# Flamingo block, two gated layers: first Toeplitz tiles read from the taps, a third buffer for turned x, weight signs spread out and moved, down products of the last stage one tile later

## The reference

```
x = x + tanh(g_xattn[0]) * conv_attention(ctx, ctx, layernorm(x))
x = x + tanh(g_ffn[0])   * ffn_A(layernorm(x))    # hidden 1408
x = x + tanh(g_xattn[1]) * attention(layernorm(x), ctx, mask)
x = x + tanh(g_ffn[1])   * ffn_B(layernorm(x))    # hidden 2048
```

## Time and profile before

| | |
|---|---|
| three runs | 777.58, 780.79, 781.33 us, median 780.79 |
| the profiled execution | 780.78 us, span 779.0 us, granted clock 0.976 of 2.4 GHz |
| TensorE | 709.3 us busy, 91% of the span |
| VectorE | 619.5 us, 80% |
| ScalarE | 373.4 us, 48% |
| GpSimd | 245.3 us, 31% |
| chain that ended last | TensorE 58%, VectorE 26%, issue 5%, ScalarE 4%, DMA 4% |

### The profile page before, as it was taken

How to read it: one execution, slowest core, us unless ns; L and a number is a source line. 1 busy time by engine, 2 the same in 40 slices (tenths; PEclk the granted TensorE clock), 3 DMA queues, 4 the chain that set the end, 5 groups by cost and what they waited for, 6 DMA issues and landing times.

```text
span 779.0 us, 9462 instructions
## 1 busy us (share of the span) xinstructions
PE 709.3 (91%) x3160; PEld 391.5 (50%) x3160; DVE 619.5 (80%) x1216; ACT 373.4 (48%) x541; POOL 245.3 (31%) x299
## 2 busy tenths in 40 slices
PE   3999999987989999977988989999999999999975
PEld 2767767765634444445654434444444444444431
DVE  1888988787989999754877698888888888888860
ACT  3154865354167778744764153334444444444430
POOL 5477687786545444232421001000000000000000
PEclk9999999999999999998999999999999999999996
DMA  7473273131049999979521034544443444333323
GB/s 258 143 269 123 61 268 117 70 93 35 7 121 220 227 204 150 218 203 318 178 82 28 1 68 81 82 82 81 82 77 73 81 82 69 74 74 65 68 60 81
DMA packets 140080, 90.97 MB, mean 117 GB/s; under 512 B 118848, under 2 KB 118848, under 8 KB 140032
## 3 DMA queue, kind: packets, MB, share of 16 engines
q1 hardware_dynamic: 138320, 86.01, 46.2%
q0 software_dynamic: 1280, 4.20, 1.8%
q10 hardware_dynamic: 432, 0.17, 0.2%
HBM read 53.04 MB, written 8.47 MB: 79 GB/s over the span
## 4 chain that ended last, share of the span: by engine, by line
PE 58%; DVE 26%; issue 5%; ACT 4%; DMA 4%; POOL 2%; SPq 1%; ACTq 0%; POOLq 0%; DVEq 0%
PE psum L732 27%; PE psum L749 14%; PE psum L614 10%; DVE phase_space L1020 3%; PE psum L693 3%; DVE phase_space L1068 3%; DVE phase_space L1029 2%; DVE a_scalars L1074 2%; DVE psum L1022 2%; DVE ln_bn L273 2%; PE psum L715 2%; DMA phase_space<-in_L_weights 2%; DVE a_scalars L1050 1%; DMA phase_space<-phase_space 1%; DVE phase_space L1035 1%
## 5 line engine op out<-in xcount | busy, mean ns | idle before, releaser
L732 PE MATMUL psum<-phase_space 128*128 128x512 f16 x1024 | 224.1, 379 | 2.8 <-DVE phase_space L1167 2.8
L614 PE MATMUL psum<-phase_space 128*128 128x288 f32 x640 | 168.7, 417 | 15.3 <-ACT phase_space L812 15.3
L732 PEld LDWEIGHTS psum<-phase_space 128*128 128x128 f16 x1024 | 100.1, 98 | 124.6 <-DVE phase_space L1167 3.8
L614 PEld LDWEIGHTS psum<-phase_space 128*128 128x128 f32 x640 | 121.1, 195 | 52.0 <-ACT phase_space L812 21.7
L749 PE MATMUL psum<-phase_space 128*128 128x512 f16 x512 | 116.0, 386 | 9.4 <-DMA phase_space<-phase_space 9.4
L589 POOL DMA_DIRECT2D out<-x_sb x16 | 9.5, 593 | 334.7 <-DVE x_sb L1200 334.7
L749 PEld LDWEIGHTS psum<-phase_space 128*128 128x128 f16 x512 | 50.7, 99 | 72.2 <-issue 13.7
L659 PE MATMUL psum<-phase_space 128*128 128x512 bf16 (+1 forms) x384 | 81.0, 366 | 5.4 <-DVE phase_space L1068 4.4
L982 ACT ACTIVATE phase_space<-psum,b_scalars 128x512 f32<-128x512 f32 x64 | 43.5, 682 | 85.3 <-PE psum L732 79.7
L988 ACT ACTIVATE phase_space<-phase_space,magic 128x1024 f32<-128x1024 f32 x32 | 36.5, 1148 | 88.9 <-DVE phase_space L1181 88.9
L284 POOL TENSOR_TENSOR ln_rs<-ln_ve,neg_half 128x1 f32<-128x1 f32 x64 | 35.8, 560 | 131.3 <-DVE ln_nm L279 130.9
(11 more groups left out here) (106 smaller groups left out, 1030.6 us busy)
## 6 DMA issues: line engine op xcount, KB each, us to landing
phase_space<-in_L_weights SPq DMA_DIRECT2D x24, 512.0 KB, 5.6
phase_space<-in_L_weights SPq DMA_DIRECT2D x12, 704.0 KB, 6.9
phase_space<-kpad SPq DMA_DIRECT2D x16, 512.0 KB, 4.2
phase_space<-in_context_heads SPq DMA_DIRECT2D x16, 384.0 KB, 4.8
...
```

The lines of the kernel that those rows point to most:

```text
L614: last = nc.tensor.matmul(at(bank(4 * hh + lo), 0, [[64, B], [1, NP]]), toep[n % 2][:, hh, (lo - li) * P:(lo - li + 1) * P], kv[n % 2][:, ...
L732: last = nc.tensor.matmul(bank(2 * (m % 3) + w), fb_qT[n % 2][:, kk % 2, kk // 2, :], b_wT[w][:, kk // 2, c * 512:(c + 1) * 512], start=(k ...
```

## The change

It has these parts.

1. Toeplitz tiles of steps 0 and 1 are loaded straight from the input taps, without waiting for `kpad`. D for their four heads is fetched (`d_first`) and added by VectorE to the diagonal of the tiles (`fold_first_d`). On GpSimd `pairs(0)` comes ahead of the first root, on ScalarE `square(0)` ahead of the norms. Tile 0 has an order of its own (`first_conv`), and x of tile 1 is turned into bank 4.
2. `q_ext` has a third buffer. `copy_q(n)` waits for the products of tile n - 3 by `s_fold`, which they count one operation earlier.
3. `a_scale_x` of the first three tiles goes ahead of head 1's products, and `fold_heads(15, 1)` behind the first two products of the feed-forward. Tile 14's down products go behind `scores(0)`.
4. Weights of B: one piece or one set of context rows per step in A, 6 signs in A instead of 13, 10 in the attention, and the last 8, those of `w3`, behind the silus of B's tiles 0 and 1. Only the first 16 are waited for before B. The mean for `w3` is made later and apart (`fb_sm` has four sets of scalars instead of two).
5. Scaling, rounding and splitting of x(0) and x(1) for B go at steps 10 to 15 one behind the other.
6. In B `b_down(n)` stands behind the chunks of tile n + 2, and `b_residual` comes one tile later. GpSimd norms x two tiles earlier.

```diff
-        q_ext = [view(R_M + k * 768, [G, 384]) for k in range(2)]
+        q_ext = [view(off, [G, 384]) for off in (R_M, R_M + 768, R_F + 5120)]
...
                 def load_toeplitz(n):
                     if n >= 2:
                         sp.wait_ge(s_y, 2 * n - 2)
-                    rows = kpad[n * G:n * G + G, :]
+                    if n == 2:
+                        sp.wait_ge(s_kpad, 16)
+                    rows = (kpad if n >= 2 else taps_in)[n * G:n * G + G, :]
...
+                load_toeplitz(0)
                 load_x(0)
                 load_x(1)
                 load_context(1)
+                load_toeplitz(1)
                 load_x(2)
-                sp.wait_ge(s_kpad, 16)
-                load_toeplitz(0)
                 load_x(3)
-                load_toeplitz(1)
...
                 for t in range(NT + 1):
                     if t < NT - 2:
                         turn_x(t + 2)
-                    if t < B:
-                        load_rows(t)
                     if t >= 1:
...
-                    if 2 <= t < NT - 1:
-                        load_b(t - 2)
+                    if t % 2 == 0 and t < NT:
+                        load_rows(t // 2)
+                    if t % 2 == 1 and 3 <= t < NT - 1:
+                        load_b((t - 3) // 2)
...
+                load_b(6)
+                load_b(7)
...
-                    if b >= 3:
-                        load_b(NT - 6 + b)
+                    if b >= 4:
+                        load_b(b + 4)
...
+                load_b(2 * PERW)
                 fb_turn_x(1)
+                for j in range(2 * PERW + 1, NBC):
+                    load_b(j)
...
-                ln_root(pool, 0, 0)
-                conv_offset(0)
                 pairs(0)
-                for n in (1, 2):
+                for n in range(3):
...
+                b_norm(2)
+                b_norm(3)
                 for n in range(NT):
-                    if n + 2 < NT:
-                        b_norm(n + 2)
+                    if n + 4 < NT:
+                        b_norm(n + 4)
...
-                        last = nc.tensor.transpose(bank4(0)[:, lb, :], xh_c[n % 2][:, lb * P:lb * P + P], ident[:, :])
+                        last = nc.tensor.transpose(bank4(4 if n == 1 else 0)[:, lb, :], xh_c[n % 2][:, lb * P:lb * P + P], ident[:, :])
...
+                def first_conv():
+                    pe.wait_ge(s_kv, 1)
+                    pe.wait_ge(s_sq, 1)
+                    pe.wait_ge(s_tfix, 2)
+                    conv_block(0, 0, 3)
+                    conv_block(0, 0, 2)
+                    turn_q(0)
+                    conv_block(0, 0, 1)
+                    pe.wait_ge(s_qc, 1)
+                    conv_block(0, 0, 0).then_inc(s_y, 1)
+                    turn_q(1)
+                    conv_block(0, 1, 3)
+                    conv_block(0, 1, 2)
+                    conv_block(0, 1, 1)
+                    pe.wait_ge(s_qc, 2)
+                    conv_block(0, 1, 0).then_inc(s_y, 1)
+
...
+                    if n == 1:
+                        pe.wait_ge(s_tfix, 4)
+                    else:
+                        pe.wait_ge(s_tp[n % 2], 16 * (n // 2 + 1))
+                    pe.wait_ge(s_prod, 2 * n - 1)
...
-                a_down_product(NT - 2)
                 c_turn_x(1)
                 for i in range(NT):
                     scores(i)
+                    if i == 0:
+                        a_down_product(NT - 2)
...
-                    if i == NT - 1:
+                    if i == NT - 2:
                         pe.wait_ge(t_red, 1)
-                        nc.tensor.matmul(bank(7)[:, 0:3], ones[:, :], tot[:, 4:7], start=True, stop=True).then_inc(t_tot, 1)
+                        pe.wait_ge(f_r, NT)
+                        nc.tensor.matmul(bank(7)[:, 0:2], ones[:, :], tot[:, 4:6], start=True, stop=True).then_inc(t_tot, 1)
...
+                pe.wait_ge(s_bs, 2 * PERW)
...
-                    if n >= 1:
...
+                    if n == 2:
+                        pe.wait_ge(s_bs, NBC)
+                    if n >= 2:
+                        b_down(n - 2)
+                    if n == 2:
+                        pe.wait_ge(t_red, 2)
+                        pe.wait_ge(t_fac, 1)
+                        nc.tensor.matmul(bank(7)[:, 2:3], ones[:, :], tot[:, 6:7], start=True, stop=True).then_inc(t_tot, 1)
+                b_down(NT - 2)
                 b_down(NT - 1)
...
-                    if n >= 2:
-                        act.wait_ge(s_prod, 2 * n - 2)
-                    src = bank(0)
-                    dst = q_ext[n % 2].rearrange("p g c -> p (g c)")
+                    if n >= 3:
+                        act.wait_ge(s_fold, 2 * n - 4)
+                    src = bank(4 if n == 1 else 0)
+                    dst = q_ext[n % 3].rearrange("p g c -> p (g c)")
...
+                square(0)
+                norm_q(0)
+                norm_q(1)
+                copy_q(0)
...
-                norm_q(0)
-                square(0)
-                norm_q(1)
-                copy_q(0)
...
-                    if t >= 3:
-                        sign_b(t - 3)
+                    if t % 2 == 1 and t >= 5:
+                        sign_b((t - 5) // 2)
...
-                    if i == 10 or i == 13:
-                        fb_round_x((i - 10) // 3)
-                    if i == 11 or i == 14:
-                        fb_high_x((i - 10) // 3)
-                    if i >= 3 and NT - 6 + i < NBC:
-                        sign_b(NT - 6 + i)
+                    if 11 <= i < 13:
+                        fb_round_x(i - 11)
+                    if 13 <= i < 15:
+                        fb_high_x(i - 13)
+                    if 3 <= i < 13:
+                        sign_b(i + 3)
...
                 for n in range(NT):
                     for c in range(NCB):
                         fb_silu(n, c)
+                        if n < 2:
+                            sign_b(2 * PERW + NCB * n + c)
...
                     y = psum[:, 4 * hh:4 * hh + 4, :].rearrange("p l c -> p (l c)")
...
-                        dve.wait_ge(s_res, 2 * NT - 2 + 2 * t)
+                    if t == 0 and c == 0:
+                        dve.wait_ge(s_res, 2 * NT - 2)
+                    if t == 1 and c == 0:
+                        dve.wait_ge(s_res, 2 * NT)
...
+                def fold_first_d(n):
+                    dve.wait_ge(s_tp[n], 16)
+                    for hh in range(G):
+                        diag = toep[n][:, hh, 0:P]
+                        nc.vector.scalar_tensor_tensor(diag, at(ident[:, :], P - 1, [[-1, P]]),
+                                                       d_first[:, n * G + hh:n * G + hh + 1], diag, ALU.mult, ALU.add
+                                                       ).then_inc(s_tfix, 1)
...
+                    if n >= NT - 3:
+                        a_scale_x(n + 3 - NT)
...
-                    fold_heads(n, 1)
-                    if n >= NT - 3:
-                        a_scale_x(n + 3 - NT)
+                    if n < NT - 1:
+                        fold_heads(n, 1)
...
                 for t in range(NT):
                     a_product(t, 0)
+                    if t == 0:
+                        a_product(0, 1)
+                        fold_heads(NT - 1, 1)
                     if t < NT - 3:
                         a_scale_x(t + 3)
-                    a_product(t, 1)
+                    if t >= 1:
+                        a_product(t, 1)
...
-                a_residual(NT - 2)
...
                 for i in range(NT):
                     masked(i)
+                    if i == 0:
+                        a_residual(NT - 2)
...
-                    if i == 10 or i == 13:
-                        fb_scale_x((i - 10) // 3)
-                    if i == 11 or i == 14:
-                        fb_deq_x((i - 10) // 3)
-                    if i == 12 or i == 15:
-                        fb_low_x((i - 10) // 3)
-                    if i == NT - 2:
-                        dve.wait_ge(s_ba, NBC)
-                        nc.vector.tensor_reduce(tot[:, 4:7], b_abs[:, :, :], AX.X, ALU.add).then_inc(t_red, 1)
-                dve.wait_ge(t_tot, 1)
-                nc.vector.tensor_scalar(b_fac[:, 0:3], bank(7)[:, 0:3], 1.0 / (FB * L), 1.0 / (QMAX * USCALE),
-                                        ALU.mult, ALU.mult).then_inc(t_fac, 1)
-                dve.wait_ge(t_fac, 1)
-                nc.vector.tensor_tensor(b_fac[:, 2:3], b_fac[:, 2:3], gates[:, 3:4], ALU.mult).then_inc(t_fac, 1)
-                fb_up_scales(0)
-                fb_up_scales(1)
+                    if 10 <= i < 12:
+                        fb_scale_x(i - 10)
+                    if 12 <= i < 14:
+                        fb_deq_x(i - 12)
+                    if 14 <= i < 16:
+                        fb_low_x(i - 14)
+                    if i == NT - 3:
+                        dve.wait_ge(s_ba, 2 * PERW)
```

(26 more changed lines are left out.)

59 lines of the change are left out of this document (31 added, 28 removed).

## The result

The changed kernel takes 749.86 us (median of 4 runs, 749.32 to 750.29), beside 780.32 us before (4 runs). The ratio is 0.9615, with a 95% interval of 0.9588 to 0.9641: 3.9% faster. The profiled execution has a span of 747.5 us, before 779.0, so 31.5 us have gone. Forecast were 751 and 30.2.

The account below looks back on a forecast made before the run. Limits differ by stage: convolution a loop through ScalarE, first feed-forward VectorE, attention four engines, last stage TensorE. Terms: -24.6 - 6.8 - 4.3 + 1.7 + 6.8 - 3.0 = -30.2 from 780.8, said as 751; own range 746 to 757, chance 0.56.

Parts of the forecast that it names:

- Start: Convolution's start: first matmul at 8.6 instead of 14.61, head 0's last part of tile 1 at 26, not 31.24; -5.2 us.
- Third buffer: Convolution, tiles 1 to 14, with the moved scale: ordinary period 10.75 us instead of 11.47; -15.3 us.
- the handover: End of convolution into first feed-forward: the slow clock behind 188.57 goes with the idle time; -1.4 us.
- Rival (a): Convolution: GpSimd comes first in every tile, lengthening head 1's folds, VectorE's tile 11.9 us; total 765; chance 0.13.
- The -6.8: Attention, to scores(11): signs use weights asked for before the reloads, so ScalarE's wait for weights goes; -6.8 us.
- The -4.3: Attention, scores(11) to scores(15): scales, roundings and parts spread over more steps lose 4.0 us instead of 8.3; -4.3 us.
- The +1.7: End of attention: x's low part comes at step 14, and the last stage's first up product waits for its transpose; +1.7 us.
- Ramp: Start of last stage: signs between silus delay x(2), TensorE idles 10.8 us behind tile 1, then runs cold; +6.8 us.
- Rival (b): Last stage's ramp costs less: x(2)'s parts come as early as before, TensorE waits 6.5 us, stays warm; 744; chance 0.08.
- Tail: End of last stage: 13.8 us of down products cover the wait, idle 9.4 becomes 2.5, last 32 matmuls take 6.91; -3.0 us.
- (e): Rival, last stage: clock stays low after the new idle of 10.8 us; slower than before, 813 at 3 tiles; chance 0.02.
- (f): Rival, whole kernel: all gains come back as waits on VectorE or for loads; no change, 781; chance 0.03.

Follow-up runs that it names:

- start_fast: Changed kernel with ScalarE's square(0) ahead of the kpad store and VectorE's fold of D into the first Toeplitz tiles ahead of the taps' fold: 747.68 us.
- start_trip: Changed kernel with the first two Toeplitz tiles loaded from kpad again, behind the taps' round trip, without D folded into them: 751.87 us.
- two_bufs: Changed kernel with q_ext at two buffers again and copy_q waiting for the last product of tile n-2: 761.04 us.
- scale_back: Changed kernel with a_scale_x of the first three tiles behind head 1's products and fold again: 754.90 us.
- loads_later: Changed kernel with the attention's first weights (piece 6) asked for behind the second reload, each later piece one place later than in an earlier try: 754.41 us.
- steps_old: Changed kernel with scaling, rounding and splitting of x(0) and x(1) at steps 10 to 12 and 13 to 15 again, signs as changed: 749.69 us.
- x2_early: Changed kernel with x(2) of the last stage scaled, rounded, split and turned during tile 0's last chunk, not tile 1's silus: 746.88 us.

## Why the prediction was right, and where its steps were not

The time, 749.86, is 1.1 us from the 751 forecast, and the likeliest case came. That it is so close is in part luck: some terms were off and cancelled.

**Start, -5.2 forecast, -3.8 measured.** The failed step is that tile 0's squares, named among what the first matmul needs, got no time in the sum. They ended at 10.16, behind D's landing, the store and the table load, and the first matmul came 1.8 us late. That ScalarE's order made a late D hold up the square is shown by start_fast: 8.38, close to the 8.6 of the text. Why D landed at 7.69, before at 5.47, is open: a Toeplitz load is now asked for ahead of it, but in start_trip, without that load, it still landed at 6.92. In both kernels the new load of `d_first` is asked for ahead of D's as well, which is asked for 0.46 us later than before; no run took that out.

**Third buffer, -15.3 forecast, -18.0 measured.** The period was mis-sized, 10.58 and not 10.75; that is 2.0 of the 2.7. It was also two causes in one term: taking back the buffer alone loses 11 us (two_bufs), the scale alone 5 (scale_back).

**"VectorE's late tiles then hold 10.6 us, still below TensorE's"** is the step that failed: -1.4 forecast for the handover, +2.2 measured. From the first product of tile 12 to that of tile 13, 14 and 15 VectorE took 11.0, 13.7 and 10.8 us, more than TensorE's 10.58, so VectorE bounds everything from 147 us on. The eight folds of tiles 12 to 15 took 9.6 us (one of them 2.92), where 0.69 each would be 5.5. This gave back part of what the period gave, which is why the two errors cancel: -16.7 forecast for both, -15.8 measured.

**Rival (a)** did not come: its rule holds, but GpSimd did not come first in every tile. Folds over 2 us, where the pairs come first, are five in the changed kernel and seven before, and from 104 to 158 us the pairs start behind the fold in six tiles in a row. But "nothing in the change alters their distance", which stood against it, was wrong too. Before, the pairs started 0.06 us behind the fold of head 1 in three late tiles in a row (123.38, 134.86, 146.33), now 0.23 to 0.25; head 1's fold went from 0.69 to 0.83 and head 0's from 0.69 to 1.17, both against GpSimd's short operations. VectorE's tile went from 9.36 (40.8 of 50 us, by 11.47) to 9.74 us (46.0 of 50, by 10.58), or, from one fold of head 1 to the next (123.38 before, 124.30 after), from 9.1 to 9.7, not to 11.9.

**Attention.** The -6.8 is confirmed by loads_later, for three quarters of it. The -4.3 has the right size, and its reason is wrong for the most part, which is luck: steps_old shows that "spread over more steps" is 0.9 of it. The +1.7 was 0.5, since the transposes landed 0.5 us after TensorE was ready.

**Ramp, +6.8 forecast, +5.0 measured.** The mechanism is the one named: 7.8 us idle behind tile 1, released by a transpose. I had 10.8. Of these 3.0 us 1.7 is that tile 1's last chunk took 5.31 us instead of 3.6, and 1.3 that x(2) came earlier. Only the 1.3 shortens the stage; with the slow clock, which cost 2.5 us and not 3, it makes up the 1.8 between the two figures. x2_early adds what I had not seen: with x(2) early, product 0 of a tile is next in line, and its waits add up to 7.95 us in place of 2.47 and 7.77. Rival (b), 744 for early parts of x(2), left it out.

**Tail, -3.0 and -3.0.** Idle 2.2 us in place of 9.4, and 16 matmuls in 3.6, as named.

**The chances.** The last sums do not fit the rivals: (e), with 0.02, is slower and (f), with 0.03, is no change, so "same 0.02, slower 0.03" has the two the wrong way round.
